# A quarter of a step's outputs is moved behind the next step's turned maxima in two attention stages of a twelve-stage decoder kernel

## What is computed

```python
# L0_xattn: 32 heads of 8 channels, 128 keys, rotated q and k
x = x + _L0_xattn_ref(_layernorm(x, axis=-1), ctx_1024, ...)
# L2_xattn: 16 heads of 16 channels; the last 16 keys form a softmax of their own
ctx = _attn(qT, k.transpose(0, 2, 1, 3), v.transpose(0, 2, 1, 3))
ctx_dca = _attn(qT, k_dca.transpose(0, 2, 1, 3), v_dca.transpose(0, 2, 1, 3))
ctx = ctx + DCA_WEIGHT * ctx_dca
```

## Time and profile before

| | |
|---|---|
| three executions | 2133.47, 2135.55, 2133.70 us, median 2133.7 |
| profiled execution | 2131.74 us, of which the span of its instructions is 2130.0 |
| mean granted TensorE clock | 0.924 of full speed |
| busy: PE, DVE, ACT, POOL | 1811.5, 1316.1, 961.3, 509.8 us |
| steps of L0x (16) | about 157 to 265 us of the span |
| steps of L2x (8) | about 1168 to 1246 us |
| steps of L0a (8, causal) | about 40 to 108 us |

### The profile page before, as it was taken

The page is one execution under the profiler, slowest core; times in us unless marked ns, Lnnn a source line. Parts: engine busy times, 40 slices in busy tenths (PEclk is TensorE's granted clock), DMA queues, the critical chain, the costliest instruction groups (busy, mean ns, idle before and its releaser), DMA issues. The chain is left out here.

```text
span 2130.0 us, 39122 instructions
## 1 busy us (share of the span) xinstructions
PE 1811.5 (85%) x14754; PEld 1472.3 (69%) x14758; DVE 1316.1 (62%) x2421; ACT 961.3 (45%) x1934; POOL 509.8 (24%) x557
## 2 busy tenths in 40 slices
PE   6877745689999789999757777799999998899798
PEld 4756622468999678888425665577778776788666
DVE  4575577456565654444476765788888886676632
ACT  2343445335555422222214324466667664455532
POOL 1020010023333433532030012344555552000100
PEclk9989966789999899999877987999999999999999
DMA  2020000020000101000100000000010012111000
GB/s 91 3 82 3 3 26 0 15 75 23 26 26 22 67 31 60 30 30 0 39 12 1 3 24 15 23 24 29 30 30 30 30 30 88 40 36 36 2 1 20
DMA packets 13501, 61.47 MB, mean 29 GB/s; under 512 B 1872, under 2 KB 2000, under 8 KB 11216
## 3 DMA queue, kind: packets, MB, share of 16 engines
q1 hardware_dynamic: 13392, 59.95, 8.2%
HBM read 58.90 MB, written 1.05 MB: 28 GB/s over the span
## 5 line engine op out<-in xcount | busy, mean ns | idle before, releaser
L2348 DVE SCALAR_TENSOR_TENSOR arena<-bank,arena 128x508 f32<-128x508 f32 (+2 forms) x204 | 151.7, 744 | 35.0 <-ACT arena L2344 23.0
L2473 PE MATMUL bank<-L3a_wo,L3a_y_gated 128*128 128x256 f32 x512 | 124.1, 387 | 0.0
L2679 DVE TENSOR_TENSOR L3a_decays<-L3a_decays,L3a_cb_masked 128x512 f32<-128x512 f32 x128 | 94.7, 802 | 43.8 <-ACT L3a_decays L2564 43.8
L2496 PE MATMUL bank<-L3a_xnT_high,L3a_w_high 128*128 128x512 f32 x256 | 106.4, 416 | 10.8 <-POOL L3a_w_low L2799 9.2
L2564 ACT ACTIVATE L3a_decays<-bank 128x512 f32<-128x512 f32 x128 | 66.1, 604 | 99.2 <-PE bank L2447 99.2
L1804 PE MATMUL bank<-L1f_xnT_high,L1f_high 128*128 128x512 f32 x256 | 101.6, 397 | 7.6 <-DVE L1f_hidden L1867 7.6
L2473 PEld LDWEIGHTS bank<-L3a_wo,L3a_y_gated 128*128 128x128 f32 x512 | 92.4, 190 | 17.7 <-issue 7.3
L218 PE MATMUL bank<-const,xn 128*128 128x128 f32 x192 | 47.3, 418 | 66.4 <-ACT xn L202 61.0
L1804 PE MATMUL bank<-L1f_xnT_low,L1f_high 128*128 128x512 f32 x256 | 101.2, 395 | 0.0
L1804 PE MATMUL bank<-L1f_xnT_high,L1f_low 128*128 128x512 f32 x256 | 101.0, 394 | 0.0
L1838 ACT ACTIVATE L1f_silu<-bank 128x512 f32<-128x512 f32 x64 | 38.3, 598 | 138.3 <-PE bank L1804 138.3
(11 more groups left out here) (571 smaller groups left out, 5298.8 us busy)
## 6 DMA issues: line engine op xcount, KB each, us to landing
arena<-in_L3p SPq DMA_DIRECT2D x32, 388.0 KB, 3.0
arena<-in_L1f SPq DMA_DIRECT2D x8, 1536.0 KB, 6.7
arena<-in_L1x SPq DMA_DIRECT2D x18, 384.0 KB, 3.0
arena<-in_L3x SPq DMA_DIRECT2D x18, 384.0 KB, 3.0
arena<-in_L0f SPq DMA_DIRECT2D x1, 4224.0 KB, 13.2
arena<-in_L3f SPq DMA_DIRECT2D x1, 4055.0 KB, 12.5
arena<-in_L2x SPq DMA_DIRECT2D x1, 1989.0 KB, 7.9
arena<-in_L0a SPq DMA_DIRECT2D x1, 1571.0 KB, 9.3
```

The source lines that it names most:

```text
L2348: return nc.vector.scalar_tensor_tensor(dst[:, :, d:], psum[:, :, 0:P - d], wcol, dst[:, :, d:], ALU.mult, ALU.add)
L2473: mm = nc.tensor.matmul(ps[g // 2][:, (g % 2) * C:(g % 2 + 1) * C], yg[:, o, g * P:(g + 1) * P], wo[:, o, :], start=False, stop=False, ski ...
L2496: mm = nc.tensor.matmul(bank(name, half)[:, :], wm[a][:, kc, :], (xh, xl)[b][:, kc, half * HALF:(half + 1) * HALF], start=(kc + at == 0), ...
L2679: nc.vector.tensor_tensor(d, d, cbm[:, 4 * half:4 * half + 4, :].rearrange("p b t -> p (b t)"), ALU.mult).then_inc(S["dec_ready"], 1)
```

## The change

values takes a function `between`, which it calls once inside its list of groups. In the causal case this is behind the last group, which is the same order as before. Without the causal mask it is behind three quarters of the groups, rounded down: behind group 6 of 8 in L2x, and behind group 1 of 2 in L0x (3 * 2 // 4 = 1), that is with half of the matmuls left. The function is turn_max(s). The first turn_max, of step 0, stands as before. No instruction is added or removed; ACT, DVE, POOL and SP keep their streams.

```diff
-    def values(self, pe, s):
+    def values(self, pe, s, between):
         b = s // self.per
         pe.wait_ge(self.s_exp, 4 * s + 4)
         chunks = range(KC) if self.per == 1 else (s % 2,)
-        for c in chunks:
-            for m in range(self.M):
-                for bank, at, w in self.outputs(s, c, m):
-                    for e in range(self.E):
...
+        parts = [(c, m, *place) for c in chunks for m in range(self.M) for place in self.outputs(s, c, m)]
+        for n, (c, m, bank, at, w) in enumerate(parts):
+            for e in range(self.E):
...
+            if n + 1 == (len(parts) if self.causal else 3 * len(parts) // 4):
+                between()
         mm.then_inc(self.s_o, 1)
...
             if s:
-                self.values(pe, s - 1)
-            if s < self.NS:
+                self.values(pe, s - 1, lambda: self.turn_max(pe, s) if s < self.NS else None)
+            else:
                 self.turn_max(pe, s)
```

More of the change, by code:

```diff
@@ L420, in values @@
         chunks = range(KC) if self.per == 1 else (s % 2,)
-        for c in chunks:
-            for m in range(self.M):
-                for bank, at, w in self.outputs(s, c, m):
-                    for e in range(self.E):
[L425 to L430, removed]
+        parts = [(c, m, *place) for c in chunks for m in range(self.M) for place in self.outputs(s, c, m)]
+        for n, (c, m, bank, at, w) in enumerate(parts):
+            for e in range(self.E):
+                slot = c * self.E + e if self.per == 1 else e
+                for r in range(4):
+                    g = slice(32 * r, 32 * r + 32)
+                    lhsT = self.v[:, m, b, c, e, g] if w else self.ones[:, m, e, :]
+                    mm = self.nc.tensor.matmul(bank[g, at], lhsT, self.pT[:, r, slot, :], start=(e == 0),
+                                               stop=(e == self.E - 1), skip_group_check=True)
+            if n + 1 == (len(parts) if self.causal else 3 * len(parts) // 4):
+                between()
         mm.then_inc(self.s_o, 1)
```

## The result

The changed kernel takes 2139.95 us as the median of 12 runs (2134.48 to 2143.94). The kernel before, timed beside it, takes 2134.61 as the median of 12 (2129.74 to 2137.94). The ratio is 1.0023, 95% interval 1.0013 to 1.0032: slower by some 5 us, interval about 3 to 7. The forecast was 2142, slower, between 2137 and 2149.

The account below looks back on a forecast made before the run. Each stage was held by a loop of waits: PE's in L0x, one of DVE, PE and ACT in L2x. L0x +2.1, L2x +5.0 and clock +1.3 gave +8.4 us on 2133.7, rounded 2142; range 2137.0 to 2149.0.

Parts of the forecast that it names:

- The loop of L2x: In L2x, two groups behind the turn delay ACT's copy and DVE's reciprocal: period 8.90 to 9.77 us, together +5.0 us.
- L0x: In L0x, PE waits for DVE's maxima before the turn: period 6.39 us in place of 6.28, together +2.1 us.
- a true quarter: In L0x, only a quarter of the outputs behind the turn (0.45 us): a gain of about 0.3 us a step.
- The clock: Granted clock falls inside L2x; two that count, less what the phase gives back: +1.3 us, ends -2.5 and +6.
- the rival in which it falls: Rival, chance 0.18: clock falls in L0x and in most steps of L2x, +5 us more, 2147 us.
- Drain both ways: Rival, chance 0.12: gaps of 0.37 us behind the turn and 0.33 ahead of the turned scores; 5.5 more, 2147.5 us.
- Almost free: Rival, chance 0.10: no gap ahead of the turned scores, last step of L2x at the high clock; 2135.7 us.
- The cover works: Rival, chance 0.05: with maxima ready sooner, L0x gives -3.8 us, and L2x -2 if PE closes its loop; 2128 us.

Follow-up runs that it names:

- L2x alone: Against the kernel before, the turn moved behind group 6 of 8 in L2x only, L0x as before; ratio 1.0023 (1.0009 to 1.0037).
- L0x alone: Against the kernel before, the turn moved behind group 1 of 2 in L0x only, L2x as before; ratio 0.9998 (0.9981 to 1.0014).

## Why the prediction was right

- **The loop of L2x.** Period forecast 9.77, measured 9.77; L495 (L494 before) 1.41 us behind the turn, forecast 1.41. The second turn comes two groups earlier, as forecast (seen in L2x alone). The linear growth with the groups, and the change of sign with the short reciprocal, show the cause: the moved turn waits for maxima, and what was put behind it holds DVE. One reading was off: PE's idle ahead of the turn, forecast as 1.9, is 2.24 us. The forecast took it from the old step, but in the new one the turn moves back by 0.87 and PE's groups only by 0.57 (1.27 - 0.70): 1.94 + 0.87 - 0.57 = 2.24.
- **L0x.** Forecast 6.39, measured 6.34, the ends of the range 6.11 and 6.67. The mechanism is the forecast one, the wait for the maxima and then the piece. The terms: first load behind the turn 0.26 (forecast 0.17), loads of the group 0.81 (forecast 0.90), change to row tiles 0.20 (forecast 0.25); 1.27 together for 1.32. One term of the sum that was mis-sized is this stage's +2.1 us: first to last turn it is +0.84 to +1.02. The forecast's remark that a true quarter behind the turn would gain about 0.3 us a step came true in its own experiment: 0.30.
- **The clock.** The forecast of falls inside L2x, of 0.8 us for one that catches the two groups, and of about two that count, was right: one of 0.85 in the changed kernel, three in L2x alone, 0.81, 0.69 and 0.46. L0x kept the high level from 174.5 to 257, so the rival in which it falls did not come. What the sum had too high is the total: +8.4 forecast, some +5 measured with 3 to 7 for the interval. Of this 1.1 to 1.3 us is L0x. The other term is what the phase of the clock gives back, 0.3 in the sum. From the last turn of L2x to the end of the stage it is 19.79 us before and in L0x alone, at a mean clock of 0.83, and 17.87 us in the changed kernel and in L2x alone, at 1.00. The moved turn costs 0.57 there, so the high level gave back 2.49 us in both traces, which the forecast had only as an end of its range (-2.5). How often that happens in other executions the traces don't say, so how the missing 3 us are shared between the two terms stays open.
- **Drain both ways** fell in L0x and L2x alike. Behind the turn the first load stands 0.26, not 0.37 us; ahead of the turned scores the idle is 0.20, not 0.33. The Trainium skill (TensorEngine Tiling (Array Packing), Key Properties) says that a change of tiling mode drains TensorE. The trace agrees so far that the loads pause at both changes, 0.12 us from the end of the turn's load and 0.20 ahead of the row tiles, the size of the cheaper rows; that the pause is a drain it doesn't show, and in the first row three loads follow without idle, though one in three of L1342's is on 128*32 tiles.
- **Almost free** fell with the 0.20 us ahead of the turned scores, though its other condition, the last step of L2x at the high level, came.
- **The cover works** was the rival on the other side. The point from which it decides is borne out by runs: it works where the maxima are ready when PE reaches the turn, in L2x by the short reciprocal or the later normalise, in L0x by a turn placed behind three quarters (0.30 us a step each time).

## What to carry to other kernels

Work put between an instruction and its reader fills a wait only if the instruction could have started earlier; if its inputs come no sooner, the move just delays whatever stands behind it. So read, ahead of such a move, when the moved instruction's inputs are ready, and who waits for the work that goes behind it: here the copy and the reciprocal of L2x. And move an instruction no further ahead than to where its inputs are ready. In L0x the turn behind three quarters of the outputs gained 0.30 us a step, and behind half of them, where it had to wait, it lost 0.06. In L2x, once the maxima were ready, the same 0.8 us of loads behind the turn gained 0.30.

## What the runs showed of the hardware

A change from 128*32 to 32*128 tiles, which the steps of the kernel before never showed without a wait, takes 0.20 us of idle weight loads at the 2.4 GHz level and 0.38 at 1.2 GHz. The first group of 16 loads behind the turn lasts 0.38 us, the next ones 0.46 and stand 0.44 from start to start. A longer idle also came with falls of the clock. Between the second and the last turn of L2x it fell only in kernels whose steps had PE idle for 2.24 us ahead of the turn (two groups behind it) or 3.11 us (four), and not at every such turn; with one group and 1.80 us of idle it held through all six steps. Each fall that caught the groups added 0.5 to 1.6 us to its step. That the idle is the cause is not shown by itself, as no run changed it alone.
